# Edge tiles of 124 edges in place of 128 in a graph layer with indirect gathers

## The reference, cut to what matters

```python
def _hconv(x, src, dst, ew, w1, b1, w2, b2, g, b):
    h = jax.nn.relu(x @ w1 + b1)
    msg = ew[:, None] * h[src]
    agg = jax.ops.segment_sum(msg, dst, num_segments=x.shape[0])
    h = agg @ w2 + b2
    return jax.nn.relu(_bn(h, g, b))
...
    h = _hconv(h0, src, dst, ew, c1...);  h = relu(_bn(h, ...))
    h = _hconv(h, src, dst, ew, c2...);   h = _bn(h, ...)
    x = x + relu(h + residual)
x = x + ffn(layernorm(x))        # top 2 of 8 experts
```

## Time and profile before

| | |
|---|---|
| median of 3 runs | 5939.43 us (5933.58 to 5940.53) |
| the profiled execution: its span | 5933.4 us, and 6.0 us of the median outside it |
| planning | 0 to 27 us |
| input projection | 27 to 192 us |
| edge stage, layer 1 | 194 to 2160 us |
| norms, hidden projection | 2162 to 2398 us |
| edge stage, layer 2 | 2399 to 4365 us |
| norms, routing, lists | 4365 to 4909 us |
| experts | 4909 to 5933 us |
| busy: PE, PEld, DVE, ACT, POOL | 4953.2, 3943.8, 3325.4, 1118.3, 3907.2 us |

### The profile page before, as it was taken

How to read it: one execution, slowest core, us unless ns; L and a number is a source line. 1 busy time by engine, 2 the same in 40 slices (tenths; PEclk the granted TensorE clock), 3 DMA queues, 4 the chain that set the end, 5 groups by cost and what they waited for, 6 DMA issues and landing times. The chain is left out here.

```text
span 5933.4 us, 96651 instructions
## 1 busy us (share of the span) xinstructions
PE 4953.2 (83%) x20263; PEld 3943.8 (66%) x20264; DVE 3325.4 (56%) x9391; ACT 1118.3 (19%) x2545; POOL 3907.2 (66%) x3930
## 2 busy tenths in 40 slices
PE   6799989899998886898899988989984755777776
PEld 5677767677776665676677766767763645666665
DVE  6555555555555556555555555555567755555554
ACT  3100000000000025000000000000037744444444
POOL 2577777777777734777777777777723764555555
PEclk9755555555555578655555555555575558999999
DMA  5333333333333321333333333333312533333333
GB/s 157 115 105 105 105 105 105 105 105 105 105 105 105 105 57 66 109 105 105 105 105 105 105 105 105 105 105 105 105 43 75 113 101 92 55 55 55 55 55 52
DMA packets 323442, 560.11 MB, mean 94 GB/s; under 512 B 101905, under 2 KB 213905, under 8 KB 323122
## 3 DMA queue, kind: packets, MB, share of 16 engines
q0 software_dynamic: 196304, 465.62, 29.6%
q1 hardware_dynamic: 114306, 81.01, 5.2%
q10 hardware_dynamic: 12768, 12.85, 0.7%
HBM read 479.80 MB, written 79.41 MB: 94 GB/s over the span
## 5 line engine op out<-in xcount | busy, mean ns | idle before, releaser
L607 PE MATMUL c_partial<-c_onehot,c_messages 128*128 128x128 f32 x12544 | 3552.2, 437 | 396.4 <-DMA c_messages<-h,c_indices 220.7
L592 POOL DMA_INDIRECT c_messages<-h,c_indices x3136 | 2964.1, 945 | 978.9 <-issue 953.7
L607 PEld LDWEIGHTS c_partial<-c_onehot,c_messages 128*128 128x128 f32 x12544 | 2767.1, 307 | 1181.7 <-DVE c_onehot L616 614.0
L635 DVE TENSOR_TENSOR sums<-sums,c_partial 128x256 f32 x3136 | 1322.2, 422 | 1784.1 <-PE c_partial L607 1776.1
L616 DVE TENSOR_SCALAR c_onehot<-iota,edge_dst,edge_w 128x128 f32<-128x128 f32 x3144 | 1089.1, 347 | 13.2 <-PEq L87 13.2
L582 ACT ACTIVATE c_indices<-edge_src 128x8 int32 x392 | 81.8, 209 | 3823.7 <-PE c_partial L607 3805.9
L1520 POOL DMA_INDIRECT out<-ffn_result,ffn_table x204 | 323.0, 1583 | 383.6 <-DMA out<-ffn_result,ffn_table 322.4
L1535 PE MATMUL ffn_ps_x<-ident,ffn_rows 128*128 128x128 f32 x416 | 90.9, 300 | 254.0 <-DMA ffn_rows<-tokens,ffn_table 251.1
L1501 POOL DMA_INDIRECT ffn_rows<-tokens,ffn_table x209 | 233.4, 1117 | 72.4 <-issue 64.0
L1676 DVE CAST ffn_xT_high<-ffn_xT 128x256 fp32r<-128x256 f32 x207 | 63.0, 304 | 372.3 <-ACT ffn_xT L1617 356.7
L1186 POOL DMA_INDIRECT table<-rt_entry,rt_slot x196 | 201.3, 1027 | 72.1 <-issue 51.9
(11 more groups left out here) (171 smaller groups left out, 4218.3 us busy)
## 6 DMA issues: line engine op xcount, KB each, us to landing
c_messages<-h,c_indices POOLq DMA_INDIRECT x3136, 2.7
pi_x<-in_x SPq DMA_DIRECT2D x14, 896.0 KB, 5.5
h<-pi_h ACTq DMA_DIRECT2D x14, 896.0 KB, 4.6
rt_x<-in_x SPq DMA_DIRECT2D x14, 896.0 KB
out<-rt_x SPq DMA_DIRECT2D x14, 896.0 KB, 13.1
tokens<-rt_tokens SPq DMA_DIRECT2D x14, 896.0 KB, 6.7
h<-ph_h SPq DMA_DIRECT2D x24, 512.0 KB, 2.9
ffn_w<-in_w SPq DMA_DIRECT2D x16, 512.0 KB, 10.4
```

Source lines behind the costliest of these rows:

```text
L592: pool.indirect_dma_start(messages[:, k, :], None, source, bass.IndirectOffsetOnAxis(ap=indices[:, k // HALF, k % HALF:k % HALF + 1], axis ...
L607: last = pe.matmul(partial[:, k % SUM_BANKS, g * P:(g + 1) * P], messages[:, k, g * P:(g + 1) * P], onehot[:, k % LEAD, :], start=True, st ...
L635: dve.tensor_tensor(where, where, partial[:, k % SUM_BANKS, 0:C].rearrange("p (g n) -> p g n", g=CG), ALU.add).then_inc(s_added, 1)
```

## The change

The width of an edge tile is a constant of its own, `W = 124`, and everything that had 128 edges in a tile has 124: the rows of the edge arrays in DRAM (496 bytes), the planning's chunks, the transposes' results, and in the edge stage the partitions of the indices, of the gather, of the one-hot tile and of both operands of the matmul. The free sizes of the edge stage stay. `EDGE_TILES` becomes 1613, `ROUNDS` 101, so 1616 steps a layer; the planning has 14 chunks of 128 tiles. The ring, its slots and the order of waits stay as they are.

```diff
+W = 124
+EDGE_TILES = -(-EDGES // W)
-EDGE_TILES = -(-EDGES // P)
... plan_tiles (and the same in plan_steps)
-        g_src = sb("g_src", [P, K, P], I32)
+        g_src = sb("g_src", [P, K, W], I32)
... g_dst, g_ew, f_src, f_dst likewise
-            link(dve.tensor_tensor(f_dst[:], g_dst[:], g_dst[:, :, 0:1].to_broadcast([P, K, P]), ALU.subtract))
-            dve.tensor_scalar(exceeds[:], f_dst[:, :, P - 1], float(P), None, ALU.is_ge).then_inc(s_float[1], 1)
+            link(dve.tensor_tensor(f_dst[:], g_dst[:], g_dst[:, :, 0:1].to_broadcast([P, K, W]), ALU.subtract))
+            dve.tensor_scalar(exceeds[:], f_dst[:, :, W - 1], float(P), None, ALU.is_ge).then_inc(s_float[1], 1)
-                dve.tensor_copy(dest[:, c0 * P:c1 * P], turned[:, g % 4, 0:(c1 - c0) * P]).then_inc(s_out, 1)
+                dve.tensor_copy(dest[0:W, c0 * P:c1 * P], turned[0:W, g % 4, 0:(c1 - c0) * P]).then_inc(s_out, 1)
-                    last = pe.transpose(turned[:, g % 4, (c - c0) * P:(c - c0 + 1) * P], rows[:, c, :], t["ident"][:])
+                    last = pe.transpose(turned[0:W, g % 4, (c - c0) * P:(c - c0 + 1) * P], rows[:, c, :], t["ident"][:])
... sum_messages
-                    act.activation(indices[:, half, :], t["edge_src"][:, bass.ds(first_step + first, HALF)],
+                    act.activation(indices[0:W, half, :], t["edge_src"][0:W, bass.ds(first_step + first, HALF)],
                                    ACT.Copy).then_inc(s_index, 1)
-                    pool.indirect_dma_start(messages[:, k, :], None, source,
-                                            bass.IndirectOffsetOnAxis(ap=indices[:, k // HALF, k % HALF:k % HALF + 1],
+                    pool.indirect_dma_start(messages[0:W, k, :], None, source,
+                                            bass.IndirectOffsetOnAxis(ap=indices[0:W, k // HALF, k % HALF:k % HALF + 1],
                                                                       axis=0)).then_inc(s_message[k], 16)
-                                         messages[:, k, g * P:(g + 1) * P], onehot[:, k % LEAD, :],
+                                         messages[0:W, k, g * P:(g + 1) * P], onehot[0:W, k % LEAD, :],
-                return dve.tensor_scalar(onehot[:, slot, :], t["iota"][:], t["edge_dst"][:, bass.ds(first_step + step, 1)],
-                                         t["edge_w"][:, bass.ds(first_step + step, 1)], ALU.is_equal, ALU.mult)
+                return dve.tensor_scalar(onehot[0:W, slot, :], t["iota"][0:W, :], t["edge_dst"][0:W, bass.ds(first_step + step, 1)],
+                                         t["edge_w"][0:W, bass.ds(first_step + step, 1)], ALU.is_equal, ALU.mult)
... kernel: the three edge arrays are padded to EDGE_ROWS * W edges
-            a = np.concatenate([a, np.zeros(pad_edges, a.dtype)]).reshape(EDGE_ROWS, P)
+            a = np.concatenate([a, np.zeros(pad_edges, a.dtype)]).reshape(EDGE_ROWS, W)
```

## The result

The changed kernel takes 7147.54 us (median of 4, 7145.40 to 7149.57) against 5939.05 us for the kernel before beside it: ratio 1.2035, 95% interval 1.2018 to 1.2052. It is 20% slower. The prediction was 6025 us with a range of 5600 to 6450: the sign was right, but only by the added gathers; the change in the time of one gather was forecast with the wrong sign.

The account below looks back on a forecast made before the run. GpSimd's gathers were taken as the bound: span 5933.4 + 120.0 (added gathers) - 33.7 (fewer rows each) - 2 (padding) + 1.5 (planning) = 6019.2 us, plus 6.0 for the runs' median, so 6025 us, range 5600 to 6450.

Parts of the forecast that it names:

- What bounds the kernel: Both edge stages: GpSimd's stream of gathers sets the pace, 3136 x 1.2497 = 3919 us, 66% of the span.
- The 96 added gathers: Edge stages, both layers: 1616 gathers a layer for 1568, at 1.2497 us each, +120.0 us.
- the time of a row: Each gather on GpSimd: 2.6 ns saved a row, 10.4 ns a gather with 4 rows fewer, 33.7 us in all.
- B: Gathers on GpSimd: 124 rows leave the form it does best, 1117 ns each, +676 us, 6615 us; chance 0.19.
- B's far end: Dearest case of the dearer gather: 1583 ns each, put at +2150 us.
- forecast: The likeliest case: added gathers less a small saving per row, 6025 us, own range 5990 to 6062; chance 0.44.
- C: Gather data on few unchanging DMA engines, 31 rows on each of four: pace 1.74 us, +1705 us, 7645 us; chance 0.06.
- The Trainium skill's rule: DMA transfers spread over the largest number up to 16 dividing the slowest dimension: 16 for 128, only 4 for 124.
- A: Gathers: instruction or gap time that isn't per row shrinks with fewer DMA engines served, -162 us, 5777 us; chance 0.26.
- D: Gathers: time is per row through and through, gap included, so -6 us, within 0.2% of before; chance 0.05.
- Later landing at no cost: Gathers landing some 1.3 us later cost nothing, since 8 to 16 ring slots are ahead, 10 us and more.
- Small terms: Fewer whole padding tiles at the layers' ends, -2 us, and a longer planning at the start, +1.5 us; these cancel.

## Why the prediction was wrong

- What bounds the kernel: right. The difference is 3232 gathers at GpSimd's pace.
- The 96 added gathers at +120 us: right. With gathers of 128 rows put back the cost is 114 us.
- **The step that failed is the time of a row.** The prediction bounded it from below by nothing and from above by 7.4 ns, "what fewer rows alone can give", and took -10.4 ns a gather. The instruction's time does not hang on the number of rows but on the rows of the busiest engine, which went from 8 to 31 as the number of rows fell: +339 ns in place of -10.4, 3232 x 0.339 = +1096 us in place of -33.7.
- The rival that came true is B, a dearer gather, chance 0.19; its price was 172 ns, from the experts' gathers, and the true one is twice that. Its reason, a form that GpSimd does worse, was not borne out: the widths that divide well over 16 engines take no more than 128. The range, cut at +511 us, missed it. (B's far end, 3232 x 1.8877 less 3919, is +2182 us and not +2150; forecast, B and C add to 0.69 and not 0.68.) "Nothing shows that it depends on the number of rows" was true of the trace and was taken as evidence against, where it was only a blank.
- The Trainium skill's rule was looked up and its 4 engines were right; it was asked whether the data fit (they did, rival C) and whether fewer engines save something (A), not what 31 rows on one engine mean for the instruction that prepares them. The indirect transfers of the trace of before all had 128 rows, 8 to a share, so the slope, (1283 - 945) / 23 = 14.7 ns a row of share, was not to be read from it. But the prediction's own two bounds could have been put on the share: from nothing to all 945 ns over 8 rows, 118 ns a row, which is 0 to +2.7 us a gather for 23 rows more. That is wide, but all of it on the dearer side, where the forecast had -10.4 ns.
- A is refuted: the gap stays at 0.30 us, every gather's packets are counted as for 16 engines, and 17 rows on one engine take 1074 ns for 1099 with 119 rows on seven, so the number of engines with data is worth 25 ns. C is refuted by a pace of 1.59 us where it asks for 1.74, with GpSimd hardly waiting for index copies. D, with its gain from fewer rows, is refuted too.
- Later landing at no cost: right in kind (4.7 us, 2.0 later in place of 1.3), no engine ahead of TensorE waits for it.
- Small terms: the tail from a layer's last gather to its last add was to give back 2 us; from the last gather to the next layer's first it gave 4 in layer 1. The loads of 496 bytes did no harm: from 4 to 8 us they run at 303 GB/s where the 512-byte rows ran at 300, and the first gather starts at 193.42 for 194.07, so the planning cost nothing that shows.

## What to carry to other kernels

Before a gather's row count is changed, find the largest number up to 16 that divides it. The times and packet counts of all 30 widths run here fit that as the number of DMA engines that share the rows, and the instruction of a gather of 1 KB rows costs some 830 ns plus 13 to 15 ns for each row of that share, not of the whole, and 12 to 48 ns more on 3 to 15 engines. Keep row counts at multiples of 16, or pad them up to one: a gather of 128 rows with four thrown away is 338 ns cheaper than one of 124. And where the fixed part is 830 of 945 ns, only fewer gathers help, not shorter ones.

## What the runs showed of the hardware that was not expected

- A gather makes as many packets as if each of 16 engines had the share of the busiest: 48 at a share of 8, 144 at 31 whether the rows are 124 or 31, small ones where there are no data (112 of 144 under 512 bytes at 124 rows).
- Gathers on 3 to 15 engines take more than those with the same share on 1, 2 or 16: 12 to 18 ns at 31 rows of share (4 and 3 engines), 22 to 25 at 17, 35 to 40 at 8 (11, 13 and 15 engines), 48 at 6 (12 engines). Why isn't shown. On 16 engines the slope falls from 24 ns for the second row of share to 11 a row between 4 and 8 (847, 871, 900, 945 ns at 1, 2, 4 and 8).
- In three of the five sets of runs, on three chips, the kernel before took 7142 to 7149 us (medians) in place of 5932 to 5939, with GpSimd, VectorE and TensorE holding each other up for up to 7 us at a time, while gathers and adds have their usual durations (948 and 419 ns). Waits of VectorE's adds and TensorE's weight loads in 500 us of it (total us, times, longest us):

```profile
DVE sums L635 <- remote: 175.9, 48, 6.4
PEld c_partial L607 <- DVE c_onehot L616: 171.9, 67, 6.1
```

  What releases the adds isn't in the trace, and the cause stays open. The edge stages of a kernel whose gathers are slow enough (1.59 us a step) don't show it.
